# First loads of a Perceiver kernel issued from two queues: half of the first weights and of the first context from ScalarE's queue

## The chip, the cores and the metric

The kernel runs on one core of a Trainium2 chip. The metric is the device time of one execution in microseconds (us). The kernel before takes 430.87 us, the median of three runs (430.41, 430.87 and 431.71).

## What is computed

One layer of a Perceiver on 8 batches of 64 latent tokens of width 512, with a context of 512 rows for each batch. Three blocks, each added to the residual `x`; the change concerns the start of the first.

```python
# x: (8, 64, 512), ctx_1024: (8, 512, 512)
x = x + xattn(layernorm(x), ctx_1024, ...)      # c = layernorm(x), q = ctx_1024
#   cq = einsum('bcd,bqd,d->bcq', c, q, w_cq) + b_cq
#   s  = (c @ w_c + b_c)[:, :, None] + (q @ w_q + b_q)[:, None, :] + cq
#   a  = softmax(s, axis=2);  c2q = einsum('bcq,bqd->bcd', a, q)
#   b_att = softmax(max(s, axis=2), axis=1);  q2c = einsum('bc,bcd->bd', b_att, c)
#   z = concatenate([c, c2q, c * c2q, c * q2c]) @ W_l.T + b_l
x = x + attn(layernorm(x), ...)     # attention, convolution over its output, attention again
x = x + ffn(layernorm(x), ...)      # 14 experts, each token goes to its two best
```

## The kernel before

The 512 tokens are four tiles `n` = 0 to 3 of 128 tokens, each of two batches `j`. The program of each engine is written out by hand, in its own order; engines wait for one another through semaphores. What matters here is the first 25 us.

- **SyncE** (SP) issues nearly all loads on its own queue, in the order of its program: tile 0 of `x` (`x_in[0]`), the two halves of the first quarter of `W_l` (`wlT`, 512 KB each, semaphores `wl_first_in[0]` and `[1]`), the transposed context `ctxT` of tile 0 (`load_ctxT(0)`: 1 MB for each of its two batches, into the buffer that the profile calls `A`), tiles 1 to 3 of `x`, the context `ctx` in plain form for tile 0 (`load_ctxN(0)`, 2 MB), and a further quarter of `W_l`. Then it waits for the scores of tile 0 before it loads `ctxT` again.
- **ScalarE** (ACT) issues two loads of 2 KB, `wcq` and `wq`, on its own queue, and then: `first_roots` (root of the variance of tile 0), `high_wl(0)` (the rounded high part of the first half of the weights), `high_first`, `high_wl(1)` (L514, waits for `wl_first_in[1]`), `copy_cT(0, 0)` (L500), `widen_first` (L508, four activations that make `cwT`, the tokens that the scores multiply), `other_roots` (L532).
- **VectorE** (DVE) normalises tile 0, makes the low parts of the weights (`low_wl`, L1072) and of the tokens (`low_part(0, 0)`, L1066), then `variance_others` (L993, L994: waits for tiles 1, 2, 3 of `x` in turn) and `normalise(1..3)` (L1001).
- **GpSimd** (POOL) makes constants and issues four small loads (`wc`, `scal`), on the queue that the profile calls software_dynamic.
- **TensorE** (PE) runs 12 matmuls on zeros (L1723), `turn_normed(0, 0)` (L1617), `project_c(0)` (L1645 to L1661, with both halves of the weights), `scores(0)` (L1633), the turns of the other tiles (L1617), and so on.

`scores(0)` begins with these waits, for all four pieces of `cwT` and for both halves of the context, which count on one semaphore:

```python
pe.wait_ge(cw_ready, KT * (n + 1))
pe.wait_ge(ctxT_in, 32 * (n + 1))
```

The lines of the profile are those of the listing below.

Of the kernel before, what the change touches and what calls it, by code (L numbers as in the profile page):

```python
# [23 lines left out]
P = 128  # L24
# [25 lines left out]
def perceiver_kernel(nc, t, out):  # L50

    ctx = ExitStack()
    with ctx:
# [9 lines left out]
        def sem(name):  # L63
            return ctx.enter_context(nc.semaphore(name))
# [37 lines left out]
        wl = w2[:, :, :].rearrange("p a (k n) -> p (a k) n", n=D)  # L102
# [15 lines left out]
        ctxT = A1[:, 0:2 * KT * Q].rearrange("p (j k q) -> p j k q", j=2, k=KT)  # L118
# [126 lines left out]
        ctxT_in, ctxN_in = sem("ctxT_in"), sem("ctxN_in")  # L245
        wl_in = [sem(f"wl_in{i}") for i in range(4)]
        wl_first_in = [sem(f"wl_first_in{i}") for i in range(2)]
# [10 lines left out]
        s_psum, nmax_ready, exp_done, r_psum = map(sem, ("s_psum", "nmax_ready", "exp_done", "r_psum"))  # L258
# [87 lines left out]
        def wl_half(i):  # L346

            at = KT * WL_ORDER[i // 2] + KT * (i % 2) // 2
            return slice(at, at + KT // 2)
# [18 lines left out]
        def _(sp):  # L368
            def load_x(n):
                sp.dma_start(x_res[:, n, :], t["x"][tile(n), :]).then_inc(x_in[n], 16)  # L370

            def load_ctxT(n):
                if n:
                    sp.wait_ge(s_psum, n)
                for j in range(2):
                    sp.dma_start(ctxT[:, j], t["ctxT"][2 * n + j]) \
                        .then_inc(ctxT_in, 16)
# [11 lines left out]
                    .then_inc(wl_in[part], 16)  # L389

            load_x(0)
            for i in range(2):
                sp.dma_start(wl[:, wl_half(i), :], t["wlT"][2 * P * i:2 * P * (i + 1), :].rearrange(
                    "(k p) n -> p k n", p=P)).then_inc(wl_first_in[i], 16)
            load_ctxT(0)
            for n in range(1, NT):
                load_x(n)
            load_ctxN(0)
            load_wl(3)
            load_ctxT(1)  # L400
            load_wl(1)
            load_wl(2)
            load_ctxN(1)
            load_ctxT(2)
            load_ctxN(2)

# [87 lines left out]
        def _(act):  # L494
            for dst, src in ((wcq, "wcqT"), (wq, "wqT")):
                act.dma_start(dst[:, :], t[src]).then_inc(widths_in, 16)

            def copy_cT(l, n):
                act.wait_ge(cT_psum, NT * l + n + 1)
                nc.scalar.activation((c_hi if l == 1 else cT)[:, :, tile(n)], turn_bank(l, n)[:, :].rearrange(  # L500
                    "p (k n) -> p k n", k=KT), ACT.Copy).then_inc(cT_ready, 1)
# [1724 lines left out]
```

## Time and profile before

| what | us |
|---|---|
| median of three runs | 430.87 |
| lowest and highest | 430.41, 431.71 |
| the profiled execution, its whole time | 432.17 |
| its span, first to last instruction | 430.6 |
| TensorE busy | 413.9 (96%) |
| VectorE busy | 329.9 (77%) |
| ScalarE busy | 216.3 (50%) |
| GpSimd busy | 62.4 (14%) |

TensorE has something to do in nearly all of the span. The page cuts the span in 40 slices of 10.8 us: in the first, TensorE is busy for 7 tenths, in most others for 9 or more. The engines' shares are sums over the whole span; what a transfer at the start is worth is read from who waits for it.

### The profile page before, as it was taken

What the parts mean: (1) busy time and instruction counts of PE and PEld (TensorE: products, weight loads), DVE (VectorE), ACT (ScalarE), POOL (GpSimd) and SP (SyncE); (2) the same over time, 40 slices, a digit from 0 to 9 for tenths busy, and PEclk for the clock granted to TensorE, in tenths of its full rate; (3) what the DMA queues carried; (4) which work ended last, traced back from release to release, by engine and by line L of the source; (5) the groups of instructions that cost most, each with busy time, mean ns of one, the idle gap of its engine ahead of it and who ended that gap; (6) DMA issues with size and microseconds to landing.
All of it is one profiled execution on the core that took longest, in us unless ns stands there. A gap on an engine that the chain in (4) does not pass through costs nothing.

```text
span 430.6 us, 8283 instructions
## 1 busy us (share of the span) xinstructions
PE 413.9 (96%) x3102; PEld 313.1 (73%) x3102; DVE 329.9 (77%) x599; ACT 216.3 (50%) x374; POOL 62.4 (14%) x84
## 2 busy tenths in 40 slices
PE   7699999999999999999989979999999999999995
PEld 3276665688898799995668745787777778777783
DVE  4458789866249883438977989899988888988656
ACT  5265225121447343122436333698778888778410
POOL 5050000000404120102102801000000000000162
PEclk9899999999999999999999999999999999999999
DMA  7999699899960360009224579899999999994662
GB/s 250 391 342 361 246 430 370 325 408 407 418 264 3 89 279 2 2 2 374 118 84 164 195 234 362 312 348 371 385 396 380 363 376 378 348 359 195 224 192 98
DMA packets 24558, 116.74 MB, mean 271 GB/s; under 512 B 2838, under 2 KB 2854, under 8 KB 18000
## 3 DMA queue, kind: packets, MB, share of 16 engines
q1 hardware_dynamic: 12992, 93.33, 56.5%
q10 hardware_dynamic: 9328, 18.09, 10.9%
q0 software_dynamic: 2208, 4.91, 3.9%
q8 instruction: 21, 0.34, 0.3%
q14 instruction: 9, 0.07, 0.0%
HBM read 94.04 MB, written 21.23 MB: 268 GB/s over the span
## 4 chain that ended last, share of the span: by engine, by line
PE 81%; DVE 7%; DMA 5%; ACT 2%; POOL 2%; issue 2%; SPq 0%; ACTq 0%; DVEq 0%
PE banks L2053 5%; PE banks L2051 5%; PE banks L2052 5%; PE banks L2084 4%; PE banks L1633 4%; PE banks L1657 4%; PE banks L2095 3%; PE banks L2094 3%; PE banks L2093 3%; PE banks L1698 3%; PE banks L1658 3%; PE banks L1661 3%; DMA A<-in_ctxT 3%; PE banks L1772 3%; PE banks L1617 3%; PE banks L1782 3%
## 5 line engine op out<-in xcount | busy, mean ns | idle before, releaser
L1400 DVE TENSOR_TENSOR w_lo<-w,w_hi 128x1024 fp32r<-128x1024 f32 x48 | 55.5, 1218 | 0.0
L682 ACT ACTIVATE w_hi<-w 128x1024 fp32r<-128x1024 f32 x48 | 47.3, 1094 | 2.3 <-DMA w<-in_w 2.3
L767 ACT ACTIVATE A<-banks,b_sb 128x128 f32<-128x128 f32 x112 | 30.4, 383 | 25.9 <-PE banks L2064 16.3
L2051 PE MATMUL banks<-w_hi,cT_r 128*128 128x512 f32 x100 | 40.1, 401 | 0.0
L2053 PE MATMUL banks<-w_hi,cT_r 128*128 128x512 f32 x100 | 39.0, 390 | 0.0
L2052 PE MATMUL banks<-w_lo,cT_r 128*128 128x512 f32 x100 | 39.0, 390 | 0.0
L923 POOL DMA_DIRECT2D b_sb<-in_b1T x12 | 6.5, 541 | 135.6 <-ACT A L767 120.2
L1503 DVE COPY A<-banks 128x512 f32<-128x512 f32 x28 | 18.0, 685 | 10.2 <-PE banks L2053 10.2
L881 POOL TENSOR_TENSOR A<-A,hrec 128x1024 f32<-128x1024 f32 x8 | 16.5, 2056 | 61.0 <-DVE hrec L1218 61.0
L1209 DVE TENSOR_REDUCE hmax<-banks 128x16 f32<-128x1024 f32 x8 | 9.8, 1221 | 18.2 <-PE banks L1847 18.2
L2053 PEld LDWEIGHTS banks<-w_hi,cT_r 128*128 128x128 f32 x100 | 18.8, 188 | 4.0
L2051 PEld LDWEIGHTS banks<-w_hi,cT_r 128*128 128x128 f32 x100 | 18.8, 188 | 3.5
L2052 PEld LDWEIGHTS banks<-w_lo,cT_r 128*128 128x128 f32 x100 | 18.8, 188 | 3.4
L2084 PE MATMUL banks<-w,A 128*128 128x512 f32 x44 | 20.7, 593 | 0.0
L1657 PE MATMUL banks<-w_lo,A2r 128*128 128x512 f32 x48 | 19.8, 413 | 0.0
L1633 PE MATMUL banks<-A 128*64 128x512 f32 x64 | 16.3, 657 | 3.5 <-DMA A<-in_ctxT 3.5
L1658 PE MATMUL banks<-w_lo,A2r 128*128 128x512 f32 x48 | 18.8, 392 | 0.0
L781 ACT ACTIVATE A2r<-w 128x1024 fp32r<-128x1024 f32 x12 | 12.1, 1053 | 11.0 <-DVE A L1541 7.1
L653 ACT ACTIVATE A<-w 128x1024 f32<-128x1024 f32 x8 | 8.5, 1060 | 18.1 <-DVE w L1210 18.1
L888 POOL TENSOR_TENSOR wqkv_lo<-wqkv,w_lo 128x1024 fp32r<-128x1024 f32 x2 | 4.8, 2395 | 83.8 <-ACT w_lo L582 83.8
L1805 PE MATMUL banks<-c_hi,w_lo 128*128 128x256 f32 x64 | 16.4, 289 | 0.0
L1806 PE MATMUL banks<-c_hi,wqkv_lo 128*128 128x256 f32 x64 | 16.0, 283 | 0.0
(370 smaller groups left out, 1048.0 us busy)
## 6 DMA issues: line engine op xcount, KB each, us to landing
w<-in_w SPq DMA_DIRECT2D x24, 2048.0 KB, 7.8
rows_dram<-A ACTq DMA_DIRECT2D x1, 14592.0 KB, 51.2
A<-in_ctxT SPq DMA_DIRECT2D x8, 1024.0 KB, 10.3
A<-in_ctx SPq DMA_DIRECT2D x8, 1024.0 KB, 8.8
w<-in_w SPq DMA_DIRECT2D x5, 1024.0 KB, 8.1
w<-in_wlT SPq DMA_DIRECT2D x3, 1024.0 KB, 15.7
wqkv<-in_wqkvT SPq DMA_DIRECT2D x1, 3072.0 KB, 15.0
w<-in_convT SPq DMA_DIRECT2D x1, 3072.0 KB, 13.7
```

The costliest lines, as they stand in the source:

```text
L682: nc.scalar.activation(w1_hi[:, u, k * F:(k + 1) * F], w1[:, u, k * F:(k + 1) * F], ACT.Copy).then_inc(hi_ready, 1)
L767: ins = nc.scalar.activation(hT[:, u, f, :], HT[f // 4][:, tile(f % 4)], ACT.Gelu, bias=b1_sb[:, u, f:f + 1])
L881: nc.gpsimd.tensor_tensor(prb[:, m % 2], prb[:, m % 2], hrec[:, m % 2, :].unsqueeze(2).to_broadcast([P, H, S]), ALU.mult).then_inc(pr_read ...
L1400: nc.vector.tensor_tensor(w1_lo[:, u, part], w1[:, u, part], w1_hi[:, u, part].bitcast(F32), ALU.subtract).then_inc(lo_ready, 1)
L1503: nc.vector.tensor_copy(hpre[:, c * 512:(c + 1) * 512], HP[u][c][:, :]).then_inc(hpre_ready, 1)
L1633: ins = mm(SC[S * j:S * (j + 1), :], cwT[:, k, n * P + S * j:n * P + S * (j + 1)], ctxT[:, j, k, :], start=(k == 0), stop=(k == KT - 1))
L1657: mm(Z[n][:, :], high[:, k, :], wl_hi[:, at, :], start=(part == 0 and k == 0), stop=False)
L1658: mm(Z[n][:, :], high[:, k, :], wl_lo[:, at, :], start=False, stop=False)
L2051: mm(HP[u][c][:, :], xr[:, 0, u, k, :], high[:, at], start=(i == 0), stop=False)
L2052: mm(HP[u][c][:, :], xr[:, 0, u, k, :], low[:, at], start=False, stop=False)
L2053: ins = mm(HP[u][c][:, :], xr[:, 1, u, k, :], high[:, at], start=False, stop=(i == KT - 1))
L2084: mm(onto, hT[:, u, f, :], w2[:, u, f * D + at:f * D + at + width], start=(f == G), stop=False)
```

## The change

The second half of the first weights and the second batch of the first `ctxT` are no longer issued by SyncE but by ScalarE, behind its two small loads and ahead of its first activation. The loads, their destinations and their semaphores are the same; each queue keeps the order of what it holds.

```diff
             def load_ctxT(n):
-                if n:
-                    sp.wait_ge(s_psum, n)
+                sp.wait_ge(s_psum, n)
                 for j in range(2):
...
             load_x(0)
-            for i in range(2):
-                sp.dma_start(wl[:, wl_half(i), :], t["wlT"][2 * P * i:2 * P * (i + 1), :].rearrange(
-                    "(k p) n -> p k n", p=P)).then_inc(wl_first_in[i], 16)
-            load_ctxT(0)
+            sp.dma_start(wl[:, wl_half(0), :], t["wlT"][0:2 * P, :].rearrange("(k p) n -> p k n", p=P)) \
+                .then_inc(wl_first_in[0], 16)
+            sp.dma_start(ctxT[:, 0], t["ctxT"][0]).then_inc(ctxT_in, 16)
             for n in range(1, NT):
                 load_x(n)
...
             for dst, src in ((wcq, "wcqT"), (wq, "wqT")):
                 act.dma_start(dst[:, :], t[src]).then_inc(widths_in, 16)
+            act.dma_start(wl[:, wl_half(1), :], t["wlT"][2 * P:4 * P, :].rearrange("(k p) n -> p k n", p=P)) \
+                .then_inc(wl_first_in[1], 16)
+            act.dma_start(ctxT[:, 1], t["ctxT"][1]).then_inc(ctxT_in, 16)
```

SyncE's instructions at the start of its program, before (-) and now (+); `w<-in_wlT` is a half of the first weights, `A<-in_ctxT` one batch of the context:

```order
 L370 DMA x_res<-in_x 128x512
-L393 DMA w<-in_wlT 128x2x512 x2
-L376 DMA A<-in_ctxT 128x2048 x2
+L391 DMA w<-in_wlT 128x2x512
+L393 DMA A<-in_ctxT 128x2048
 L370 DMA x_res<-in_x 128x512 x3
-L383 DMA A<-in_ctx 128x2048 x2
```

Tiles 1 to 3 of `x` now stand in SyncE's queue behind one half of the weights and one batch of `ctxT`, no longer behind both.

ScalarE's instructions at the start of its program before:

```order
L496 DMA wcq<-in_wcqT 128x4
L496 DMA wq<-in_wqT 128x4
L525 ACT_TABLE_LOAD
L525 ACTIVATE steps<-eps 128x1
L527 ACTIVATE sd<-mv,eps 128x1
L514 ACTIVATE w_lo<-w 128x1024
```

and now:

```order
L494 DMA wcq<-in_wcqT 128x4
L494 DMA wq<-in_wqT 128x4
L495 DMA w<-in_wlT 128x2x512
L497 DMA A<-in_ctxT 128x2048
L526 ACT_TABLE_LOAD
L526 ACTIVATE steps<-eps 128x1
```

Two issues of loads came in ahead of the first table load; what follows is in the order of before.

## Rows read from the trace of the kernel before

**Rows 1.** The chain that ended last, start to 24 us: start, us, what.

```profile
1.43 0.43 SPq L393
1.90 0.46 SPq L393
...
2.92 12.79 DMA A<-in_ctxT
15.85 5.35 PE banks L1633 x16
```

**Rows 2.** Timeline, 0 to 22 us: start, us, engine, line, operation, [idle before <- releaser].

```profile
1.91 1.28 ACT L525 ACT_TABLE_LOAD   x1 [1.78 <-PEq L2216]
3.39 2.31 SPq L370 DMA_DIRECT2D x_res<-in_x  x3
...
4.70 0.29 ACT L527 ACTIVATE sd<-mv,eps 128x1 f32<-128x1 f32 x1 [1.29 <-DVE mv L987]
...
8.16 1.06 ACT L514 ACTIVATE w_lo<-w 128x1024 fp32r<-128x1024 f32 x1 [0.46 <-DMA w<-in_wlT]
...
8.72 0.39 PE L1646 MATMUL banks<-w_lo,A2r 128*128 128x512 f32 x1
...
11.14 1.20 PE L1661 MATMUL banks<-w_lo,A2r 128*128 128x512 f32 x4
...
15.85 5.35 PE L1633 MATMUL banks<-A 128*64 128x512 f32 x16 [3.52 <-DMA A<-in_ctxT]
16.38 0.69 DVE L993 BATCH_NORM_STATS2 st<-x_res 128x6 f32<-128x512 f32 x1 [5.30 <-DMA x_res<-in_x]
...
19.76 1.46 DVE L1001 TENSOR_SCALAR cn<-x_res,mv,rstd 128x512 f32<-128x512 f32 x3
```

**Rows 3.** DMA issues, each asked for at its own time: KB, us from issue to landing.

```profile
wq<-in_wqT ACTq DMA_DIRECT2D x1, 2.0 KB, 3.8
w<-in_wlT SPq DMA_DIRECT2D x1, 512.0 KB, 4.0
w<-in_wlT SPq DMA_DIRECT2D x1, 512.0 KB, 6.2
x_res<-in_x SPq DMA_DIRECT2D x1, 256.0 KB, 13.0
x_res<-in_x SPq DMA_DIRECT2D x1, 256.0 KB, 13.1
```

**Rows 4.** Stretches: length, busy of PE, PEld, DVE, ACT, POOL, PEclk, DMA share, GB/s.

```profile
5.43:8.00 2.57, 1.54 (x8) 0.66 (x6) 2.09 (x2) 1.65 (x2) 1.78 (x4) 1.00 1.04 375
8.00:11.50 3.50, 2.81 (x10) 1.50 (x11) 1.83 (x2) 3.19 (x6) 0.00 (x0) 1.00 0.64 228
11.50:15.71 4.21, 0.83 (x4) 0.35 (x2) 0.00 (x0) 0.00 (x0) 0.00 (x0) 1.00 1.01 405
...
78.00:106.00 28.00, 28.00 (x148) 21.69 (x147) 19.49 (x56) 5.78 (x11) 0.00 (x0) 1.00 1.05 408
112.00:116.00 4.00, 4.00 (x32) 3.82 (x31) 0.00 (x0) 1.96 (x5) 3.59 (x2) 1.00 1.01 432
```

**Rows 5.** DMA queues, 112 to 116 us: packets, MB, share of 16 engines.

```profile
q1 hardware_dynamic: 65, 1.60, 92.6%
q10 hardware_dynamic: 64, 0.13, 8.4%
```

**Rows 6.** DMA queues, 8 to 11.5 us.

```profile
q1 hardware_dynamic: 113, 0.79, 56.3%
q0 software_dynamic: 102, 0.00, 8.1%
```

**Rows 7.** Stretches of L1633 alone, scores of tiles 0 and 1: PE, PEld, PEclk, DMA.

```profile
15.85:21.30 5.45, 5.35 (x16) 1.76 (x16) 0.69 1.00 415
37.50:41.20 3.70, 3.63 (x16) 1.04 (x16) 1.00 1.00 421
```

**Rows 8.** A stretch, all engines, after the fall of TensorE's clock.

```profile
16.50:19.50 3.00, 3.00 (x10) 1.15 (x8) 2.51 (x6) 0.28 (x1) 0.00 (x0) 0.50 1.01 427
```

## The prediction

> **What bounds the kernel now.** I first read the chain of work that ended last, because a load counts only where somebody waits for it. It begins with SyncE's issues and goes at once to the landing of `ctxT`: issued at 2.92 us, landed at 15.71. Then `scores(0)` runs on TensorE from 15.85, and from there TensorE is the chain [rows 1]. The timeline shows the wait itself: TensorE had finished `project_c(0)` at 12.34 (11.14 + 1.20) and stood idle for 3.52 us until `ctxT` came [rows 2]. So what the change can give or take is the start of `scores(0)`. It passes to the end nearly one for one, since TensorE's work follows without a gap.
>
> Second, the issues. SyncE had issued the halves of the weights at 1.43 and 1.90 and the second batch of `ctxT` at 2.92 [rows 1], when the queue was still busy with the first half of the weights, which landed at 1.43 + 4.0 = 5.4. The second half landed at 1.90 + 6.2 = 8.1, tile 1 of `x` at 3.39 + 13.0 = 16.4, tile 3 at about 17.6 (the three issues fill 3.39 to 5.70, the last begins near 4.5, and it lands 13.1 later) [rows 2, 3]. Issue is therefore not late: what makes `ctxT` late is the moving of bytes.
>
> Third, the rates. The transfer engines moved 375 GB/s from 5.43 to 8.00, only 228 (share 0.64) from 8.00 to 11.50, and 405 after that [rows 4]. In the slow stretch GpSimd's queue has 102 packets of next to no bytes among 113 of SyncE's queue [rows 6].
>
> **The change, part by part.** *ScalarE's two more issues.* They cost ScalarE some 0.46 us each, as SyncE's did [rows 1], or up to 0.77 (2.31 for three, rows further down SyncE's queue) [rows 2]. Its table load moves from 1.91 to 2.8 or 3.5 and ends at 4.1 or 4.7; the root L527 ran at 4.70 and has 0.4 us of slack at the one price and is 0.2 late at the other [rows 2]. What covers even that is the wait for the second half of the weights, which comes later in ScalarE's order. I count nothing.
>
> *SyncE's removed issues* give nothing by themselves, as shown.
>
> *The order in which bytes come.* This is the whole of the change. The stretch with both hardware queues active shows how they share: from 112 to 116 us q1 moved 65 packets and q10 64, though q1's carry 1.60 MB and q10's 0.13 MB [rows 5]. The queues take turns packet by packet, whatever a packet holds. Both together move 432 GB/s there, and one queue alone 408 for 28 us [rows 4]: two queues are hardly faster. A packet is one contiguous row here: `ctxT` is 128 rows of 8 KB, half of the weights 256 rows of 2 KB, a tile of `x` 128 rows of 2 KB.
>
> The small load `wq` took 3.8 us [rows 3] and so held ScalarE's queue until about 5.2, nearly when SyncE's reaches its own `ctxT`. From there the 256 packets of the second half of the weights alternate with 128 of SyncE's `ctxT` and 128 of tile 1 of `x`, and then the 128 packets of ScalarE's `ctxT` with the 128 of tile 2. Hence:
>
> - The second half of the weights now has 1.05 MB of `ctxT` and 0.26 MB of `x` with it. From 5.4 on 0.52 + 1.05 + 0.26 = 1.83 MB: 0.96 MB by 8.00 at 375, and the other 0.87 at 228 GB/s in 3.8 us, so 11.8 for the mean engine. The same sum for before gives 6.8 and the trace 8.1, since the last of the 16 engines trails by 1.3. I take **13.1** (11.8 if nobody trails), where it was 8.1.
> - ScalarE's `ctxT` waits for all that stood before it and for tiles 1 and 2 of `x`, 0.52 MB more: at 405 GB/s 1.3 us. So **17.0** instead of 15.71.
>
> *What follows from the later weights.* `high_wl(1)` started at 8.16 and `project_c(0)` ended at 12.34, 4.2 us later, with ScalarE's copies and `widen_first` done within that time [rows 2]. From 13.1 this chain ends at 17.3. So a cover of before (weights early, `ctxT` late) is gone: both conditions of `scores(0)` come at about the same time, 17.0 and 17.3. It starts at **17.3, 1.5 us later** than 15.85. If the weights come at 11.8 it is 17.0 (+1.2); if they trail by the 2.1 us that `ctxT` does (2.62 MB by the same rates give 13.6, the trace 15.71), 13.9 and 18.1 (+2.3).
>
> *TensorE's clock.* `scores(0)` took 5.35 us at a mean granted clock of 0.69, `scores(1)` 3.63 at 1.00 [rows 7]: the grant was at its lower level, 1.2 of 2.4 GHz, in the 3.0 us from 16.50 to 19.50, after TensorE had been idle from 12.34 to 15.85 [rows 2, 8]. In the changed kernel the idle time moves: it lies between the first half of the projection, which ends at 9.1 (8.72 + 0.39) [rows 2], and the weights' second half at about 14, and what follows (8 matmuls until 17.3) is in front of the scores. I expect the clock to fall earlier and the slow time to be spent in part on the projection. Ends: all of the scores slow, 5.35; none, 3.6. I take the middle of the two, **4.4**, as nothing in the trace tells where it recovers. The scores then end at 21.7 instead of 21.20: **+0.5 us**.
>
> *What comes after the scores.* L1617 needs the normalised tile 1, and VectorE starts L1001 at 19.76, 3.4 us after tile 1 of `x` landed [rows 2]. Tile 3 keeps its 17.6 or so (all bytes in front of it are the same), and then come 0.7 of statistics and about 0.6 until L1001: about 19, ahead of the scores' end. The loads behind that keep their place too, since no byte was added in front of them.
>
> *Sum.* 1.5 (start) - 0.95 (clock) = +0.5 us on the profiled execution, 432.17 to 432.7. That execution is 1.3 above the median of the runs, so some of the runs may not have had the slow stretch of the clock in the scores; the same step on the median gives **431.4**.
>
> The Trainium skill (DMA: Bandwidth & Descriptors, "Queues, rings and completion order") says that a DMA engine drains a whole packet of some 9 to 17 descriptors from one ring before it turns to the next. Read against rows 5, where each row of 24 KB alternates with one of 2 KB, the measured turn is one row. By the page's turn each engine's 8 rows of `ctxT` would be one turn, and my estimate is that only tile 1 of `x` would pass in front of the second batch: 16.4 in place of 17.0.
>
> **Rivals.**
>
> - *Slower: the weights are last and the clock is slow through the scores.* For it: the 1.3 and 2.1 us by which the last engine trails. Scores from 17.3 to 18.1 and 5.35 us long: ends 22.7 to 23.5, +1.5 to +2.3, so 432.4 to 433.2. It decides once the second half of the weights lands after 12.8 (17.0 less 4.2). Against it: the clock may have recovered by then.
> - *Faster: the second queue fills idle engines.* From 8.00 to 11.50 a share of 0.36 lay idle, 1.3 us of work [rows 4], while SyncE's queue had all its loads in hand. If an engine that stalls on one ring can serve the other, or the last engine does not trail (up to 2.1), `ctxT` lands at 15.7 down to 13.6 in spite of `x`. The next bound is then tile 3 of `x`: turns from about 19.5 at best instead of 21.2 (the end of the scores now, 15.85 + 5.35). With the clock recovered this gives -1 to -2, 429 to 430. Against it: the rate with two queues, 432 against 408 [rows 4].
> - *No change: the two queues share the engines so evenly that nothing moves.* If ScalarE's `ctxT` started as early as SyncE's, with no tile of `x` before it, all lands at 15.7 as before: 430.9. Against it: packets take turns and the weights' half has twice as many of them [rows 5]. The skill says as much in the same page, "Issuing engines are not separate DMA queues": loads from several engines run on the same 16 DMA engines and only issue time is saved. By that rule, the trace agrees: issue time was off the path here [rows 1, 3].
>
> **How the numbers follow.** My forecast 0.40 (own range 430.7 to 432.1), the slower rival 0.27, the faster 0.21, no change 0.12. About 0.3% (1.3 us) is what a measurement of this kernel can tell from nothing: 429.6 to 432.2. Faster takes 0.2 from the faster rival; slower takes most of the slower rival and the edge of my own case, 0.33; the rest, 0.47, is the same. The range reaches to 429.3 below and to 433.2 above.
>
> **What would show it.** Landing of the second half of the weights at 12 to 14 instead of 8.1, and of the later `ctxT` near 17; TensorE idle between L1646 and L1649; L1633 starting at 17 to 17.5, and its mean clock. Wrong would be the whole sum if the weights land by 9 (queues do not alternate by packet) or if the DMA share in 8 to 11.5 is near 1.

## The result, and the profile after

The changed kernel takes 434.09 us (median of 5 runs, 433.61 to 434.90) against 430.87 for the kernel before: ratio 1.0069, 95% interval 1.0041 to 1.0096. It is slower by 3.2 us; forecast were 431.4 and a range to 433.2. Two slow executions further down, more than 1.5% above the fastest of their kernels (435.79 us of the kernel before, 437.14 of f3), are left out of the ratios and of the groups of runs. The profiled execution took 434.58 us with a span of 433.0, against 432.17 and 430.6 before.

The chain of work that ended last in the changed kernel, from the start (start, us, what):

```profile
1.43 0.45 ACTq L494
1.88 0.03 issue
1.90 11.86 DMA w<-in_wlT
13.77 0.02 issue
13.79 1.06 ACT w_lo L515
14.86 0.04 issue
14.90 1.22 PE banks L1650 x2
16.12 0.04 issue
16.16 1.22 PE banks L1653 x2
17.38 1.71 PE banks L1662 x4
19.09 4.42 PE banks L1634 x16
23.50 1.46 PE banks L1618 x12
```

Where `ctxT` stood in [rows 1] now stands the second half of the first weights. It lands at 13.77 us (8.1 before), and the whole of ScalarE's and TensorE's work on it follows on the path: `high_wl(1)`, eight matmuls of the projection in 4.2 us, and only then the scores of tile 0 (L1634, formerly L1633), 3.2 us later than before. They end at 23.50 instead of 21.20. From there on the two traces run side by side: the matmuls start 2.30 us later at 28, 2.30 at 77, 2.30 at 198 and 2.33 at 424 us.

Two timeline rows show the new wait and the end of `project_c(0)`'s first half:

```profile
8.86 0.40 PE L1647 MATMUL banks<-w_lo,A2r 128*128 128x512 f32 x1
13.79 1.06 ACT L515 ACTIVATE w_lo<-w 128x1024 fp32r<-128x1024 f32 x1 [5.79 <-DMA w<-in_wlT]
14.90 1.22 PE L1650 MATMUL banks<-w_lo,A2r 128*128 128x512 f32 x2 [5.64 <-ACT w_lo L515]
```

TensorE's idle time grew from 3.52 [rows 2] to 5.64 us and moved forward. The DMA issues, each asked for by itself (KB, us from issue to landing):

```profile
A<-in_ctxT SPq DMA_DIRECT2D x1, 1024.0 KB, 7.5
w<-in_wlT ACTq DMA_DIRECT2D x1, 512.0 KB, 11.9
A<-in_ctxT ACTq DMA_DIRECT2D x1, 1024.0 KB, 14.4
```

SyncE's batch of the context is in at 9.4 (1.90 + 7.5), the 512 KB of weights issued at the same moment only at 13.8, and ScalarE's batch at 16.8 (2.43 + 14.4). The reason stands in the count of packets per queue, here from 5.5 to 7.5 us:

```profile
q1 hardware_dynamic: 70, 0.57, 80.3%
q10 hardware_dynamic: 64, 0.13, 19.3%
```

70 packets of SyncE's queue to 64 of ScalarE's, with 0.57 MB against 0.13: the turns by packet of [rows 5], now in the stretch that matters. Last, stretches of all engines (length, busy of PE, PEld, DVE, ACT, POOL, PEclk, DMA share, GB/s):

```profile
8.00:11.50 3.50, 1.20 (x4) 0.67 (x4) 0.00 (x0) 0.01 (x1) 0.00 (x0) 0.86 0.56 205
11.50:15.71 4.21, 0.81 (x2) 0.50 (x2) 0.83 (x1) 1.82 (x3) 0.00 (x0) 0.50 1.02 421
14.90:19.02 4.12, 4.08 (x9) 2.31 (x9) 3.98 (x7) 2.08 (x5) 0.00 (x0) 0.50 1.03 433
19.02:23.50 4.48, 4.48 (x18) 1.30 (x18) 2.00 (x6) 1.78 (x3) 0.00 (x0) 0.81 0.80 319
```

The slow stretch of the transfer engines is as it was (share 0.56, 0.64 in [rows 4]): the second queue filled none of it. The whole rest of the projection ran with the clock at its lower level (0.50, 1.2 GHz), and the scores at 0.81.

### The profile page after: what moved, and what is told of

The parts are those of the page before. It is cut to its first block, busy times and chain, and to the rows that moved or that the text cites. A ratio compares the mean times of both kernels' runs of the same rounds, so it can differ in the third digit from the quotient of the medians.

```text
span 433.0 us, 8283 instructions
## 1 busy us (share of the span) xinstructions
PE 415.1 (96%) x3102; PEld 314.0 (73%) x3102; DVE 329.7 (76%) x599; ACT 216.3 (50%) x374; POOL 62.3 (14%) x84
## 4 chain that ended last, share of the span: by engine, by line
PE 81%; DVE 7%; DMA 4%; ACT 3%; POOL 2%; issue 2%; ACTq 0%; DVEq 0%
PE banks L2052 5%; PE banks L2054 5%; PE banks L2053 5%; PE banks L2085 4%; PE banks L1662 4%; PE banks L1634 4%; PE banks L1658 4%; PE banks L2096 3%; PE banks L2095 3%; PE banks L2094 3%; PE banks L1699 3%; PE banks L1659 3%; PE banks L1773 3%; PE banks L1618 3%; DMA w<-in_wlT 3%; PE banks L1783 3%
## 5 line engine op out<-in xcount | busy, mean ns | idle before, releaser
L1504 DVE COPY A<-banks 128x512 f32<-128x512 f32 x28 | 18.0, 685 | 10.3 <-PE banks L2054 10.2
L2085 PE MATMUL banks<-w,A 128*128 128x512 f32 x44 | 20.7, 593 | 0.0
L782 ACT ACTIVATE A2r<-w 128x1024 fp32r<-128x1024 f32 x12 | 12.1, 1053 | 11.0 <-DVE A L1542 7.1
L654 ACT ACTIVATE A<-w 128x1024 f32<-128x1024 f32 x8 | 8.5, 1060 | 18.1 <-DVE w L1211 18.1
L662 ACT ACTIVATE A<-banks 128x512 f32<-128x512 f32 x16 | 8.6, 593 | 14.4 <-PE banks L1857 14.4
```

What stands on the lines that cost most here:

```text
L1504: nc.vector.tensor_copy(hpre[:, c * 512:(c + 1) * 512], HP[u][c][:, :]).then_inc(hpre_ready, 1)
L2085: mm(onto, hT[:, u, f, :], w2[:, u, f * D + at:f * D + at + width], start=(f == G), stop=False)
```

## The experiments

Each was timed in rounds beside the kernel before, whose medians in the three comparisons were 430.7, 431.4 and 430.9 us. "Half speed" below is the time that an execution's TensorE clock spent at its lower level, worked out from its mean granted clock c and span s as 2 (1 - c) s; in the profiles up to 2.7 us of it lie at the very end, where they cost nothing. The rest lies in one or two stretches of 3.4 to 10.2 us each.

**e1: only the weights.**

```diff
             sp.dma_start(ctxT[:, 0], t["ctxT"][0]).then_inc(ctxT_in, 16)
+            sp.dma_start(ctxT[:, 1], t["ctxT"][1]).then_inc(ctxT_in, 16)
...
-            act.dma_start(ctxT[:, 1], t["ctxT"][1]).then_inc(ctxT_in, 16)
```

> Only the second half of the first weights goes through ScalarE's queue; both batches of the first context stay with SyncE. Theory (the queues take turns row by row, and the late weights are what the start waits for): its 256 rows of 2 KB now alternate with all 256 rows of 8 KB of the two contexts, so it lands last of all, at 15 to 16 us instead of 13.8, and the scores of tile 0 start 4.2 to 5.2 us behind it, near 20.5; time 435 to 436.5. Rival (the queues share by bytes, the moved context is the loss): the weights land by 10 and the time is that of the kernel before, 431.

435.34 us (ratio 1.0107, 1.0076 to 1.0137). The weights landed at 13.99, earlier than I expected but with the last of the context (13.9), and the scores ran from 19.31 to 23.51:

```profile
1.91 12.08 DMA w<-in_wlT
19.31 4.20 PE banks L1634 x16
```

So moving the weights alone gives the whole loss.

**e2: only the context.**

```diff
+            sp.dma_start(wl[:, wl_half(1), :], t["wlT"][2 * P:4 * P, :].rearrange("(k p) n -> p k n", p=P)) \
+                .then_inc(wl_first_in[1], 16)
             sp.dma_start(ctxT[:, 0], t["ctxT"][0]).then_inc(ctxT_in, 16)
...
-            act.dma_start(wl[:, wl_half(1), :], t["wlT"][2 * P:4 * P, :].rearrange("(k p) n -> p k n", p=P)) \
-                .then_inc(wl_first_in[1], 16)
```

> Only the second batch of the first context goes through ScalarE's queue; both halves of the weights stay with SyncE. Theory (late weights): the weights alternate with the moved context and land near 11 to 12 us (1.57 MB from 5.4 at the rates of before, and the trailing engine), both contexts are in by 15.7 since no tile of x passes them, the scores start at 16 to 17; time 431.5 to 433. Rival (the moved context, with x in front of it, is the loss and not the weights): 434, as the changed kernel.

433.07 us (1.0050, 1.0028 to 1.0073), just above the upper edge. The weights land at 10.7, SyncE's batch of the context at 16.2 (2.40 + 13.8), and the chain no longer passes through them. It goes through tile 1 of `x`, which trailed to 16.83:

```profile
2.92 13.91 DMA x_res<-in_x
16.85 0.70 DVE st L994
17.79 0.71 DVE st L994
18.74 0.70 DVE st L994
20.82 1.57 PE banks L1618 x12
```

That is the next bound behind the scores which the prediction had named, statistics of `x` and then the turns. It had put them at 19.5 at best, counted from the landing of tile 3; here they start at 20.8, counted from tile 1, whose statistics come first.

**e3: rows of 4 KB.** The same bytes of the first weights, laid out so that each half, on either queue, has 128 rows of 4 KB (shown for ScalarE's).

```diff
-            act.dma_start(wl[:, wl_half(1), :], t["wlT"][2 * P:4 * P, :].rearrange("(k p) n -> p k n", p=P)) \
+            act.dma_start(wl[:, wl_half(1), :], t["wlH"][1]) \
...
+        "wlH": by_partition(np.asarray(L0_xattn_W_l).T[:D].reshape(2, 2 * P, D)),
```

> The changed kernel with the first quarter of the weights laid out in memory so that each half is 128 rows of 4 KB instead of 256 of 2 KB; the bytes and queues are the same. Theory (a turn is a row whatever it holds): half as many turns, so that the second half lands with the first batch of the context and one tile of x no longer passes: weights at about 12 instead of 13.8, context at 16.2 instead of 16.8, scores from 16.5 to 17.3 instead of 19.0; time 431.5 to 432.7. Rival (sharing by bytes, or the rate of the engines is the matter): no change, 434.1.

431.86 us (1.0017, 0.9990 to 1.0044), where the changed kernel has 434.1. The chain and, from 5.5 to 7.5 us, the packets:

```profile
1.91 10.64 DMA w<-in_wlH
12.56 1.06 ACT w_lo L515
17.86 4.00 PE banks L1634 x16
```

```profile
q1 hardware_dynamic: 66, 0.54, 70.2%
q10 hardware_dynamic: 57, 0.23, 28.9%
```

Nearly the same number of packets in the same time, but 0.23 MB on ScalarE's queue instead of 0.13. The weights land at 12.55, and the scores start at 17.9, later than I expected, since the projection again runs at half speed. About two thirds of the loss go with nothing changed but the length of a row (in the profile the scores end 1.6 us sooner, 21.86 against 23.50), and the interval no longer excludes the time of the kernel before. Sharing by bytes is out.

**e4: the gap filled.**

```diff
+                    for _ in range(22):
+                        mm(Z[1][:, :], zero_bf[:, :], zero_bf[:, :].unsqueeze(1).to_broadcast([P, KT, P]), start=True, stop=True)
                     pe.wait_ge(wl_high, 2)
```

> The changed kernel with 22 matmuls on zeros on TensorE where it waits for the second half of the weights (they write a bank that is overwritten later). Theory (part of the loss is the clock: the projection behind the gap and the first of the scores run at 1.2 GHz): the clock stays at its upper level, the projection from 14.9 to the scores takes 3.3 instead of 4.2 us and the scores 3.6 instead of 4.5; 1.5 to 2 us less than the changed kernel, 432.2 to 432.7. Rival (the clock's level costs nothing here, other engines set the pace): 434.1.

432.48 us (1.0032, 1.0008 to 1.0056). The weights are as late as ever (13.9), but:

```profile
13.91 1.06 ACT w_lo L515
14.99 1.24 DVE w_lo L1073
16.27 0.72 PE banks L1655 x2
17.00 1.08 PE banks L1664 x4
18.07 3.58 PE banks L1634 x16
```

The projection ends at 18.1 instead of 19.1, the scores take 3.58 instead of 4.42 us. The clock is worth 1.8 us of the scores' end in the profiles, and 1.6 to 2.1 in the medians.

**b1, b2 and a1: both kernels again, unchanged.**

> The kernel before, unchanged, for another profile of it. The profiled execution of before took 432.17 us, the median of its runs 430.9. Theory: in most executions TensorE's clock does not fall to 1.2 GHz in the scores of tile 0, or the last DMA engine trails by less; a profile near the median then shows the scores of tile 0 ending near 20 instead of 21.2 us, and the turn of tile 1 behind them starting at 20.3 or so. Rival: the difference lies elsewhere in the span, and the scores end at 21.2 again.

> The kernel before, unchanged, a third profile of it. Its two profiles so far took 432.17 and 434.25 us beside medians of 430.9 and 431.5, and had the scores of tile 0 slow (5.35 and 6.58 us). Theory: an execution near the median has the scores at 3.6 us or one slow stretch fewer later in the span, and is 1.5 to 3 us shorter. Rival: the profiled execution is always longer, by the profiling itself.

> The changed kernel, unchanged, for a second profile. Theory (weights last, then a projection and scores partly at 1.2 GHz): weights land at 13.5 to 14, the projection ends near 19, the scores at 23 to 23.6, the time is 433.6 to 434.9. Rival (the first profile was an exception): the scores start by 17.3.

Medians 431.53, 431.61 and 434.57 us (the last 1.0081, 1.0057 to 1.0104). The profiled executions took 434.25, 433.00 and 434.38. In b1 the scores of tile 0 were slower than ever, and TensorE's clock fell once more at 219 us (L1633 alone, then all engines):

```profile
15.10:21.80 6.70, 6.58 (x16) 1.90 (x16) 0.56 1.02 421
```

```profile
215.00:223.00 8.00, 6.89 (x87) 4.12 (x86) 5.25 (x21) 2.70 (x5) 0.00 (x0) 0.79 0.01 2
```

All three profiles of the kernel before took longer than its medians, and in all three the scores were slow. How often that is so can be read from the clocks of its 90 timed runs in the three comparisons:

| half speed, us | runs | median, us |
|---|---|---|
| 0 to 2.6 | 23 | 429.9 |
| 3.4 to 6.0 | 46 | 430.9 |
| 8.6 to 10.4 | 15 | 432.2 |
| 12.1 to 13.0 | 6 | 434.4 |

The first profile had 5.2 us by its clock, with 3.4 of it in the scores, so it belongs to the second and largest group; b2 (9.5) and b1 (12.1) belong to the two dear ones. A timed run doesn't tell where its slow stretch lies, but only the first group has no room for one ahead of the end. Of the changed kernel's 15 runs none is under 9 us, with a median of 12.1. So the part of b1's and b2's theory that a slow stretch fewer saves 1 to 2 us fits the clocks; that an execution near the median has fast scores isn't shown, and no profile of the kernel before caught them fast. That profiling itself makes the kernel dear I can't exclude for the kernel before, but a profiled f1 and f3 below were cheap. a1 repeats the after: weights at 13.3, scores from 18.6 to 22.4.

**f1, f2, f3: can the start be made shorter?** f1 puts 14 matmuls on zeros ahead of `scores(0)` in the kernel before. f2 moves GpSimd's four small loads:

```diff
             for n in range(1, NT):
                 load_x(n)
+            sp.dma_start(wc[:, :], t["wcT"]).then_inc(score_params_in, 16)
+            for i, name in enumerate(("b_cq", "b_c", "b_q")):
+                sp.dma_start(scal[:, i:i + 1], t[name].to_broadcast([P, 1])).then_inc(score_params_in, 16)
             load_ctxN(0)
...
-            pool.dma_start(wc[:, :], t["wcT"]).then_inc(score_params_in, 16)
-            for i, name in enumerate(("b_cq", "b_c", "b_q")):
-                pool.dma_start(scal[:, i:i + 1], t[name].to_broadcast([P, 1])).then_inc(score_params_in, 16)
```

f3 does that and puts 8 such matmuls ahead of the scores.

> The kernel before with 14 matmuls on zeros on TensorE ahead of the scores of tile 0, where it waits for the context. Theory (the clock falls only because TensorE stands idle): the scores take 3.6 us in every execution and end at 19.5; the turns behind them then wait for the normalised tile 1 until 20.3; 0.9 us less than the profiled execution of before, and 0 to 0.7 less than its median: 430.2 to 430.9. Rival (the fill costs power or delays the scores): 431.5 or more.

> The kernel before with GpSimd's four small loads (wc and three of scal) issued by SyncE behind the tiles of x instead. Theory (they cause the stretch from 8 to 11.5 us with the engines at 0.64 of their time): the DMA share stays near 1 there, the context lands 1 to 1.3 us sooner, at 14.5, and tile 1 of x too; the scores start at 14.6 and the turns behind them at 19.0 to 19.3; 1.5 to 2 us less, 429 to 429.5. Rival (the slow stretch is there whoever loads, or moves with the small loads): no change, 430.9.

> Both: the four small loads by SyncE behind x, and 8 matmuls on zeros ahead of the scores of tile 0. Theory: as with the small loads alone, with the clock at its upper level in the scores in every execution; 428.5 to 429.5. Rival (no idle stretch long enough is left once the context comes sooner): the same as with the small loads alone.

f1: 432.56 us (1.0024, 0.9998 to 1.0050), f2: 434.31 (1.0051, 1.0017 to 1.0084), f3: 431.82 (1.0024, 0.9990 to 1.0058). All three times are misses, and the intervals of f1 and f3 don't tell them from the kernel before. f1's scores end at 18.4, and what it then waits for is tile 1 of `x`:

```profile
3.40 11.71 DMA x_res<-in_x
19.11 1.62 PE banks L1617 x12
```

In the profile f1's matmuls run 1.94 us ahead of those of before from 24 to 198 us, lose 1.3 us of it around a gap of 1.1 us at 204 in which TensorE waits for nothing that the profile shows, and the median shows no gain at all. In 11 of its 12 runs it has under 6 us at half speed, and they take 432.5, 1.7 us more than the like runs of before; seven of them have 3.4 us or more, so the fill didn't keep every execution free of a slow stretch. What makes f1 dear stays open.

f2's mechanism was as expected and its time was not. Its stretches, and its chain from 17 us:

```profile
8.00:11.50 3.50, 3.07 (x12) 2.02 (x12) 1.82 (x2) 2.87 (x6) 0.00 (x0) 1.00 0.99 414
11.50:15.71 4.21, 3.38 (x17) 1.26 (x16) 2.33 (x5) 0.00 (x0) 0.00 (x0) 1.00 0.63 217
```

```profile
17.22 17.94 DMA w<-in_wlT
35.18 1.06 ACT w_lo L517
36.27 2.36 DVE w_lo L1072 x2
```

The slow stretch of [rows 4] goes with the small loads: share 0.99 where it was 0.64, and 0.63 behind, where they now are. The context lands at 12.55 instead of 15.71 (15.0 in b1 and b2), where 14.5 was expected, and the scores end at 16.34, 4.9 us sooner. All of it is lost at 35 us, where the later quarters of the weights have not landed: bytes, not TensorE, bound that stretch once the start is short. TensorE then stood idle, and its clock fell from 39.5 to 46.3 us.

**a2: the changed kernel with the small loads by SyncE,** the edit of f2.

> The changed kernel with GpSimd's four small loads issued by SyncE behind the tiles of x. Theory (they cause both the slow stretch of the engines and the one engine that trails, and the row-by-row turns remain): the weights land at 10.5 to 11.5 instead of 13.8 with no engine trailing, the context at 13.5 to 14.5; the scores start at 15 to 16 and end at 19 to 20; behind them the later weights land at 34 to 35 as with the same edit of the kernel before, so the time is 430.5 to 433. Rival (the second queue itself makes an engine trail): weights at 13 or later.

432.65 us (1.0037, 1.0015 to 1.0059), as expected. The weights land at 10.7 and the context at 14.2; the scores run from 15.98 to 19.98:

```profile
1.91 8.76 DMA w<-in_wlT
10.68 1.06 ACT w_lo L518
15.98 4.00 PE banks L1634 x16
```

So the weights at 13.8 are not the second queue's doing alone: 3.1 us of their lateness come with GpSimd's small loads. Without them the second queue makes the weights 3.0 us late (10.7 against 7.7 in f2), with them 5.7 (13.8 against 8.1).

**h1: f3 with the later weights first.**

```diff
-            load_ctxT(1)
             load_wl(1)
             load_wl(2)
+            load_ctxT(1)
```

> The kernel before with the small loads by SyncE behind x, the 8 matmuls on zeros, and the next two quarters of the weights issued ahead of the context of tile 1 instead of behind it. Theory (with the start 4.6 us sooner, the next bound is the landing of those quarters, 34.4 us): they land at 27 to 29 and the lead of 4.5 us over the profiled execution of before is kept; 427 to 428. Rival (the bytes bound this stretch, and the context of tile 1 becomes the late one): 429 to 430, as without the new order.

435.19 us (1.0097, 1.0060 to 1.0134), worse than its rival. The scores of tile 1, which before took 3.63 us [rows 7]:

```profile
37.52 5.29 PE L1633 MATMUL banks<-A 128*64 128x512 f32 x16 [3.81 <-issue]
```

The weights came in time and the context of tile 1 did not. The view names no releaser, but the last of its landings stands in the trace at 37.4, next to the start at 37.52: TensorE waits 3.81 us for it and comes back at half speed. No version tried beats the kernel before.

## Why the prediction was wrong, point by point

| step | predicted | measured in the profile |
|---|---|---|
| queues take turns by packet | 1 : 1 | 70 : 64 |
| second half of the weights lands | 13.1 | 13.8 |
| later context lands | 17.0 | 16.8 |
| from the weights to the scores | 4.2 | 5.3 |
| scores start | 17.3 | 19.1 |
| length of the scores | 4.4 | 4.4 |
| scores end, beside 21.20 | +0.5 | +2.3 |

- **The order of the bytes was right**, and so was the loss of cover: the weights became the last condition. e1, e2 and e3 show each part.
- **The step that failed is TensorE's clock.** The sum credited it with -0.95 us, because the slow time would "be spent in part on the projection", as if that cost nothing there. But in the same sum the projection had become the path. At half speed its second half takes 4.2 us instead of 3.1 (e4), so the chain from the weights to the scores is 5.3 long. I took its length, 4.2, from a trace in which it ran at full speed, and put the slow stretch into it in the next sentence. The missing term is 1.1 us.
- **A size was off too.** The weights came at 13.8 and not at 13.1: the term for the last engine's trailing, 1.3, was 0.7 short. The two together are 1.8 us, the whole difference between the forecast +0.5 and the +2.3 at the scores' end. That the scores took the 4.4 us forecast is luck: it was the middle between two ends, and the same kernel had 3.79 in a1.
- **The base stood too high.** The step was worked out on the profiled execution and applied to the median, 1.3 us lower. The two profiles differ by 2.4 us, the medians by 3.2 and 3.7. The clock doesn't explain the 1.3: the profiled execution had 5.2 us at half speed, and the runs of before with 3.4 to 6.0 us have a median of 430.9. Its context landed at 15.71, in b1 and b2 at 15.0; the rest stays open.
- **The sizes put together.** Among executions without a slow stretch, e4's take 432.3 (7 runs) and those of before 429.9, so the lateness is worth 2.4 us. The profiles of e4 and f1, which have none either, also differ by 2.4 us from 24 us on. The prediction had +1.5. The clock costs the changed kernel 1.8 us (23.50 less 21.66, e4), and the usual run of before 1.0 (430.9 less 429.9); the balance is +0.8, where the prediction had -0.95. Together 3.2; the two measurements of the changed kernel gave 3.2 and 3.7. The clock alone is not the cause, since e4 keeps 2.4 us of the loss without any slow stretch. These sums take it that the matmuls on zeros cost nothing themselves. f1's unexplained 1.7 us leave a doubt, though e4's profile holds its distance to before within 0.1 us from 22 to 226 us.
- **The slower rival came closest, in part by luck.** Its condition, weights past 12.8, came true. Its end of the scores, 22.7 to 23.5, did too, but by another way: it had the scores at 5.35 us behind a projection at full speed, and measured were 4.42 behind one at half speed. Its time, up to 433.2, was too low because it too was put on the median.
- **The faster rival** fell: the share in the slow stretch stayed at 0.56, and f2 shows that its cause is GpSimd's small loads. **No change** fell as well. By the page's turn of 9 to 17 descriptors (the Trainium skill, DMA: Bandwidth & Descriptors, "Queues, rings and completion order") the row length of e3 would, by my estimate, have mattered little: each engine's 16 or 8 rows of half of the weights are one or two turns either way. The trace does not agree; the 70 and 64 packets, and e3, show turns of one row.

Open: what costs f1 its lead outside the profile, why e1 takes some 1 us more than the changed kernel with the same start, and why e2, whose turns start 1.0 us sooner than e3's (20.82 against 21.86), takes 1.2 us longer in the median. Differences of about 1 us between medians are thus not all read from the start of the kernel.

## What to carry to other kernels

Two hardware queues added next to no bandwidth here (432 GB/s against 408), but they change who is served when: a load with short rows gets few bytes per turn beside one with long rows, so the first thing that is needed should not be the one with the short rows on the second queue. When a wait moves, price everything behind it at the clock that the new idle time leaves, and take the cover of the old wait away from each step that it hid. Before a profile is used as the base of a sum, compare its time and its granted clock with those of the timed runs, and compare runs that have as much slow time.

## What the runs showed of the hardware

- Four loads of 0.5 to 2 KB from GpSimd's queue held the transfer engines at 0.64 of their time for 3.5 us (228 GB/s), and with them gone the context landed at 12.55 (f2), 3.2 us sooner than in the first profile of before and 2.4 sooner than in b1 and b2. Issued by SyncE behind `x` they cost a like stretch (0.63) at another place.
- From two hardware queues the engines took one row of each in turn, whether the rows had 8 KB and 2 KB (70 to 64 packets, after) or 8 KB and 4 KB (66 to 57, e3).
- An idle stretch of 2.9 us ahead of the scores (12.2 to 15.1, b1) went with 6.8 us at 1.2 GHz (14.2 to 21.0), one of 3.5 us (12.3 to 15.9, the first profile of before) with 3.4 us (16.2 to 19.6), and one of 5.6 us (9.3 to 14.9, after) with a fall from 10.5 to 20.7. The length of the idle stretch alone doesn't tell the length of the fall. With the gap filled (e4) no fall came there.
- In some executions the clock also falls for 3.4 us between 217 and 222 or between 252 and 259 us, and costs 0.9 to 1.7 us there. The groups of runs of before, from 429.9 to 434.4 us in the median, differ by their time at half speed.
